# A two-layer decoder kernel: 154 matrix products that nobody reads, placed in the order of TensorE's steps

## What is computed

```
x = _layernorm(x + _L0_attn_ref(x, w_qkv, w_proj))               # Nystrom attention, 16 heads, 64 landmarks
x = _layernorm(x + _L0_xattn_ref(x, ctx, ...))                   # cross attention, 16 heads of 8
x = _layernorm(x + _L0_ffn_ref(x, Wr, br, W1, b1, W2, b2))       # 8 experts, the best one for each token
x = _layernorm(x + _L1_attn_ref(x, Wq, Wk, Wv, Wo, bo))          # causal self attention, 16 heads of 8
x = _layernorm(x + _L1_xattn_ref(x, ctx, ctx, mask, ...))        # cross attention, 16 heads of 64, masked
x = _layernorm(x + _L1_ffn_ref(x, fc1_A, ..., fc2_logits))       # FFN, weights composed of 32 primitives
```

## Time and profile before

| | |
|---|---|
| median of 3 runs | 2523.96 us (2521.96 to 2525.28) |
| span of the profiled execution | 2520.2 us |
| mean granted TensorE clock over the span | 0.953 |
| instructions in the profile | 95538 |
| PE busy | 2266.3 us (90%) |
| DVE busy | 1956.9 us (78%) |
| ACT busy | 1450.1 us (58%) |
| POOL busy | 387.1 us (15%) |

### The profile page before, as it was taken

How to read it: one execution, slowest core, us unless ns; L and a number is a source line. 1 busy time by engine, 2 the same in 40 slices (tenths; PEclk the granted TensorE clock), 3 DMA queues, 4 the chain that set the end, 5 groups by cost and what they waited for, 6 DMA issues and landing times.

```text
span 2520.2 us, 95538 instructions
## 1 busy us (share of the span) xinstructions
PE 2266.3 (90%) x40576; PEld 1846.1 (73%) x40576; DVE 1956.9 (78%) x6166; ACT 1450.1 (58%) x5093; POOL 387.1 (15%) x530
## 2 busy tenths in 40 slices
PE   6789999999999999999999999999999999999875
PEld 3677777777777777777777777777777777777764
DVE  3568888888888888788888888788888888888652
ACT  3346666656656655656656565665656566566531
POOL 2101111111111111111111111111111111111110
PEclk9889999999999999999999999999999999999885
DMA  4200000000000000000000000000000000000000
GB/s 192 90 7 9 5 7 9 9 9 9 9 5 7 9 9 8 9 5 8 8 9 9 9 9 5 8 8 9 9 9 9 5 7 9 9 9 8 6 3 2
DMA packets 29960, 35.75 MB, mean 14 GB/s; under 512 B 3544, under 2 KB 28128, under 8 KB 28384
## 3 DMA queue, kind: packets, MB, share of 16 engines
q1 hardware_dynamic: 29536, 29.65, 3.4%
HBM read 27.54 MB, written 2.10 MB: 12 GB/s over the span
## 4 chain that ended last, share of the span: by engine, by line
PE 52%; DVE 28%; ACT 15%; issue 4%; POOL 0%; DMA 0%; SPq 0%; POOLq 0%; DVEq 0%; ACTq 0%
PE ps L477 29%; PE ps L480 8%; ACT probs L1062 5%; PE ps L744 4%; DVE probsT L1349 3%; PE ps L828 3%; ACT probs L1047 3%; PE ps L876 2%; ACT ey L985 2%; DVE x_rows L1211 2%; DVE small L1252 2%; PE ps L761 2%; PE ps L665 2%; DVE qk_v L1337 1%; DVE p L1254 1%
## 5 line engine op out<-in xcount | busy, mean ns | idle before, releaser
L1102 POOL TENSOR_TENSOR small<-small,weights 128x1 f32<-128x1 f32 x256 | 149.0, 582 | 1142.7 <-DVE small L1200 1142.7
L1010 ACT ACTIVATE probs<-ps,small 128x128 f32<-128x128 f32 x1024 | 286.1, 384 | 31.0 <-DVE small L1342 29.5
L1349 DVE COPY probsT<-ps 128x512 f32<-128x512 f32 x384 | 263.1, 685 | 36.3 <-PE ps L480 32.7
L480 PE MATMUL ps<-weights,probs 128*128 128x128 f32 x1536 | 256.1, 292 | 32.8 <-ACT probs L1010 15.4
L1342 DVE TENSOR_REDUCE small<-ps 128x4 f32<-128x512 f32 x384 | 254.2, 683 | 20.5 <-PE ps L828 10.7
L1113 POOL TENSOR_TENSOR probs<-probs,small 128x256 f32<-128x256 f32 x128 | 108.7, 849 | 885.6 <-DVE small L1478 885.6
L480 PEld LDWEIGHTS ps<-weights,probs 128*128 128x128 f32 x1536 | 178.7, 146 | 86.3 <-ACT probs L1010 44.6
L929 ACT COPY x_T<-ps 128x128 f32<-128x128 f32 x128 | 34.1, 267 | 302.9 <-PE ps L480 302.9
L1062 ACT ACTIVATE probs<-ps,small 128x128 f32<-128x128 f32 x512 | 181.6, 375 | 20.5 <-DVE small L1342 19.0
L477 PE MATMUL ps<-wz,ss 64*64 64x72 f32 x6144 | 157.4, 229 | 32.5 <-DVE wz L1294 32.4
L1293 DVE SCALAR_TENSOR_TENSOR wz<-ey,ss 128x256 f32<-128x256 f32 x320 | 142.0, 444 | 51.1 <-ACT ss L970 36.9
(11 more groups left out here) (199 smaller groups left out, 5400.0 us busy)
## 6 DMA issues: line engine op xcount, KB each, us to landing
weights<-in_wpack SPq DMA_DIRECT2D x3, 1759.0 KB
fc_A<-in_b SPq DMA_DIRECT2D x2, 2048.0 KB, 14.3
fc_A<-in_a SPq DMA_DIRECT2D x2, 2048.0 KB, 11.4
x_in_T<-in_xT SPq DMA_DIRECT2D x32, 64.0 KB, 1.8
x_in_rows<-in_x SPq DMA_DIRECT2D x32, 64.0 KB, 1.8
ctx_T<-in_ctxT SPq DMA_DIRECT2D x32, 64.0 KB, 1.9
ctx_rows<-in_ctx SPq DMA_DIRECT2D x32, 64.0 KB, 1.9
mask_i<-in_mask SPq DMA_DIRECT2D x32, 64.0 KB, 1.9
```

What stands on the lines that cost most here:

```text
L480: return nc.tensor.transpose(dst, src, ident)
L1010: ins = nc.scalar.activation(probs(s, g)[:, j], bank(s, SCORE_BANK[g], 128 * j, 128), ACT.Exp, bias=sm(s, "nb", 4 * g + j, 1), scale=-1.0)
L1102: nc.gpsimd.tensor_tensor(sm(s, out), sm(s, ve), w("mhalf"), ALU.pow).then_inc(sem(done, s), 1)
L1349: V.tensor_copy(probsT(s, n % 4).rearrange("p a b -> p (a b)"), bank(s, 2)).then_inc(sem("pT", s), 1)
```

## The change

`KEEP_FIRST` and `KEEP_LAST` name steps of a (stream, batch) and a count. Before such a step `keep_clock` issues that many products whose result no instruction reads. The first list works until lane 1 begins batch 1: each product is an fp32 128x128 of `ident` and `n_q` into bank `ps1`, which is free until then. The second works after lane 1 has begun batch 31, its last: each is a bf16 product of `ident_bf` and `causal_bf` over 512 columns into `ps2`, which is free by then. Counted in the two programs, the first list gives 68 products at 37 places and the second 86 at 42 places, 154 in all: TensorE has 21962 products and transposes where it had 21808. No wait, no semaphore and no instruction of another engine changes.

```
+KEEP_FIRST = {
+    (0, 0): (
+        "r1.t0 3  r1.v0 1  r1.t2 1  r1.v2 1  r1.y0 2  r1.y1 2  rm.gate 2  rm.drop 3  r.ln2 2  r2.s01 3  "
+        "r2.t0 1  r2.s23 1  "),
+    (NYS, 0): (
+        "n.a0 3  n.a2 1  n.b0 2  n.e3T0 3  n.W0 2  n.S1 2  n.W1 1  n.S2 1  n.W2 3  n.S3 1  n.W3 3  n.S4 2  "
+        "n.W5 2  n.z 1  n.out 1  n.ln 1  "),
+    (NYS, 1): (
+        "n.v 1  n.a0 1  n.b0 4  n.e3T0 2  n.col0 4  n.y0 1  "),
...
+}
+KEEP_LAST = {
+    (0, BATCHES - 2): (
+        "r2.v2 1  r2.out 1  r2.y1 2  r.ln3 1  ry.q1 1  ry.t0 1  ry.t1 1  ry.v1 2  ry.v2 2  r.ln4 4  "),
+    (1, BATCHES - 1): (
+        "r1.t1 7  r1.t2 2  r1.t3 1  r1.v2 3  r1.ctxT 3  r1.z 1  r1.y0 1  r1.y1 2  rm.h0 2  rm.h1 2  rm.y0 4  "
+        "rm.y2 1  rm.y3 1  r2.t1 5  r2.v0 1  r2.v1 2  r2.s23 1  r2.t2 2  r2.t3 4  r2.v2 1  r2.z 5  r2.y1 1  "
+        "r.ln3 1  ry.xT 2  ry.s01 2  ry.t2 3  ry.t3 4  ry.v3 1  ry.out 1  r.ln4 1  rf.h 1  rf.out 2  "),
+}
...
-    def run(engine, nystrom, rest, start=None):
+    def run(engine, nystrom, rest, start=None, before=None):
...
-        for _, lane, _, _, name in order:
+        for _, lane, number, _, name in order:
+            if before is not None:
+                before(lane, number, name)
             got = next(streams[lane])
...
-        run("pe", nystrom, rest, start)
+        first = {key: dict(steps(text)) for key, text in KEEP_FIRST.items()}
+        last = {key: dict(steps(text)) for key, text in KEEP_LAST.items()}
+        reached = set()
+
+        def keep_clock(lane, number, name):
+
+            if lane >= 0:
+                if (1, 1) not in reached:
+                    for _ in range(int(first.get((lane, number), {}).get(name, 0))):
+                        one(bank(1, 2, 0, 128), ident, w("n_q"))
+                if (1, BATCHES - 1) in reached:
+                    for _ in range(int(last.get((lane, number), {}).get(name, 0))):
+                        one(bank(NYS, 1).rearrange("p (a b) -> p a b", a=4), ident_bf[:], every(causal_bf[:], 4))
+                reached.add((lane, number))
+
+        run("pe", nystrom, rest, start, keep_clock)
```

More of the change, by code:

```diff
@@ L151 @@
     ),
+}
[8 more added lines that the diff above has]
+        "n.v 1  n.a0 1  n.b0 4  n.e3T0 2  n.col0 4  n.y0 1  "),
+    (NYS, 2): (
+        "n.proj 2  n.a3 1  n.b1 1  "),
+}
[3 more added lines that the diff above has]
+    (1, BATCHES - 1): (
[3 rows of a table added]
 }
```

## The result

| | median us | lowest to highest | runs |
|---|---|---|---|
| before | 2522.03 | 2509.20 to 2528.17 | 8 |
| changed | 2505.49 | 2504.08 to 2513.87 | 8 |

The ratio is 0.9949 [0.993, 0.9967], some 13 us less: faster, by an interval that excludes 1. The medians differ by more, 16.5 us, than the means of the same runs, 13.9. The profiled execution of the changed kernel took 2506.76 us with a span of 2504.8, which stands against 2520.2 before. So 2.0 us lie outside the span, as in every run that lists both, and not the 3.8 that the prediction took.

A forecast was written before the change was run, and what follows sets the result against it. TensorE, busy for 90% of the span, was taken as the bound, at half clock in stretches at both ends. Tail -6.8 and start -0.3 made -7.1 us: 2517 us, range 2507 to 2530.

The forecast's parts named there:

- held share: Part of each slow stretch's possible gain expected at full clock: in the tail all, half and a third; start a third.
- The tail, -6.8: Last batches: three slow stretches give 2.6, 2.6 and 3.9 us, products cost 2.3; at most 19.4 us to gain.
- First stretch, -2.6: 2404.8 to 2411.6 us: seven products just ahead of the clock's fall hold it wholly, gaining 2.6 us.
- Second, -2.6: 2445.8 to 2466.2 us: products ahead of the fall and behind it hold half of 5.1 us, gaining 2.6.
- Third, -3.9: 2469.7 us to the end: clock falls at unfilled waits of `ry.t0` and `ry.t1`; a third of 11.7 us gained, 3.9.
- Cost, +2.3: Last batches: products that don't fit into idle time cost half of an upper bound of 4.5 us.
- The start, -0.3: First batches: 1.8 us gained from 152 to 169 us, less 1.5 us for the products.
- Mask products count for less than fp32 ones: TensorE's clock: bf16 mask products raise it less than fp32 products, read from stretches at 2452.4 and 2462.9 us; no size given.
- The rule of long gaps: Rival: only long idle gaps, left open, lower the clock; nothing gained, 3.8 us paid, 2528 us; chance 0.06.
- Tail held almost whole: Rival: the tail gains 19.4 us less 2.3 of cost, the start 3, giving 2504 us; chance 0.12.
- The middle, 4 us to both sides: Between the ends: not touched, but a shift at the start may add or remove slow stretches, 4 us either way.

The follow-up runs named there:

- e2: The kernel before with only the last list, 86 mask products in the last two batches: 0.9971 of before, 2513.02 us.
- e4: As e2, but each mask product uses 32 of its 128 rows, with as many columns: 1.0023 of before, 2524.53 us.
- e5: The changed kernel measured once more, against the kernel before in the same session: 0.9953, 2508.09 us.
- e1: The kernel before with only the first list, 68 fp32 products in the first batches: 1.0 of before, 2522.16 us.
- e3: As e2, but with an fp32 128x128 product in place of each mask product: 0.9982 of before, 2516.33 us.
- e6: The changed kernel with 10 mask products added ahead of `ry.t0` and 5 ahead of `ry.t1` of batch 31: 0.9957 of before.
- e11: The changed kernel with 39 more mask products in the waits of batch 31: 0.9918 of before, 2497.32 us.

## Why the prediction was right, and too small

**Direction and mechanism.** Right. The price of the products was taken as 3.8 us and the clock as worth 10.9 (2.6, 2.6, 3.9 and 1.8); the runs give 4.1 to 5.6 and, by 0.0106 and 0.0124 more clock, 16 to 19, both by the slope of the line (by the tail's own rate both are some 3 us less). The net of -7.1 became -12 to -13. What was too small is the held share. The two lists run apart add up to the -7 that was forecast, so part of the rest may be spread.

**The tail, -6.8.**
- First stretch, -2.6 (2404.8): 2.5 between the marks, and 1.00 all through.
- Second, -2.6 (2445.8), half held: 3.1 between the marks. What remains is 3.4 us, not half of 20.4.
- Third, -3.9 (2469.7), a third held: 6.3. This is the term that was mis-sized. I had the clock fall at the waits of `ry.t0` and `ry.t1`, and it was at 0.50 there (1.12 us at 2469.70). But I let it stay low from there but for a rise behind `ry.t3`, and it came up at 2479.7 already, fell three times more and rose twice. The pieces at full clock hold `ry.out` (2.05 us in place of 3.78): 21.5 of 35 us are at 0.50.
- Cost, +2.3: only 1.1 (0.5 and 0.6) are seen as a loss between marks; `e2` has 3.5 above the line (1.7 by the tail's own rate), inside the bounds of 0 and 4.5, and `e4`, where the clock follows little, 7.3 against the upper bound of 9.0. The bounds held, and the half isn't refuted.

In all, the tail gives 10.8 in the profile of the change, 10 in `e5`'s and 7 in `e2`'s timed runs, around a forecast of 6.8.

**The start, -0.3.** The change's profile has -4.1, `e5`'s -2.7, `e1`'s +0.5, and `e1` is timed at 1.0 with a cost of 3.8. I had taken 1.5 for it; 3.9 was the upper bound that I gave for a clock that stays where it was, and the list's clock gain is small (0.0016), so 1.5 was too low. The stretch at 66.7 us did stand as it was, as I had said. -0.3 is right for the list alone; with the last list there were some 5 us more that I can't assign, and that two standard errors would cover.

**"Mask products count for less than fp32 ones."** Not borne out. `e3` replaces them and is not faster. What I read from the earlier trace rows was one stretch with score products on 32 rows beside mask products; `e4` shows that products on 32 rows count for less. I gave the mask products the discount that belonged to the scores, which I take for the reason why the held shares were too small; no run shows that step by itself.

**The rule of long gaps (2528).** It failed as forecast: the outcome isn't 2528. The Trainium skill ("TensorE: Matmul & The Clock Gate", "Why this matters for your kernels") has the clock lost in idle gaps of over about 3 us. The change leaves the wait of 3.45 us open and still gains. The trace has the clock at 0.50 at the end of that wait, as the rule says, but it also fell at 2448.9, 2483.1 and 2493.3, at the end of waits of 1.78, 2.57 and 1.98 us. With the long wait filled (`e6`) the tail of one profile is 7 us shorter, though the timed ratio is not. So such a gap does matter to the clock, but as one of several.

**Tail held almost whole (2504).** The time came out near this rival's for another reason: the tail still has 38.7 us at half clock. `e11` is this rival made true, and it is at 2497.

**The middle, 4 us to both sides.** In the change it moved by 0.5. But over the runs it varies by 20 us (2170.8 to 2190.4 without pauses), which is the spread of single runs. My 4 us were too few, and that it was "not touched" holds only for this number of products: 29 more ahead of it cost 50 us.

## What to carry over

Where an engine's clock is at half in the tail and its steps stand on the path that ends last, products that nobody reads are worth their price if they work on all rows and fill the waits whole: 39 more of them (`e11`) were worth 8 to 9 us on top of the change. Read their effect from the times and the mean clock of many runs, beside runs of the kernel before in the same session, not from two profiles, since single runs spread by more than the effect. And count what you add ahead of a long loop: look for waits without a releaser that repeat once in each turn, and take as many products away as you put in.

## What was not expected

- Equal time on TensorE is not equal worth for the clock: 86 products of 32 rows left the tail at 137.0 us and the kernel 5.8 us slower, 86 of 128 rows made it 125.6 and 7 us faster; both kinds take 0.42 to 0.43 us at half clock, and the mean clock rose by 0.0025 against 0.0075.
- 58 records more ahead of the middle make 27 to 28 pauses of up to 1.6 us, one in each batch, and a kernel 2.1 to 2.3% slower (1.6% with the filled tail); records of 8 columns do it as well as full ones.
- The span of this kernel follows its mean granted clock, 15 us for 0.01 (67 runs, correlation -0.94), which is 0.30 us for each us at half clock; the clock of one kernel varies from 0.949 to 0.963 between runs.
